# A decoder layer in one kernel: the cross-attention mask as three bf16 rows of the key and query stacks

## The reference

```python
# self attention
scores = einsum('bhqd,bhkd->bhqk', q, k) / sqrt(16)
scores = scores + log_pen[:, None, :, :]
ctx = einsum('bhqk,bhkd->bhqd', softmax(scores), v)
# cross attention (mask has the shape 4 x 1 x 1 x 512, one value per key)
logits = einsum('bhqd,bhkd->bhqk', q, k) / sqrt(16)
logits = logits + mask * -1000000000.0
ctx = einsum('bhqk,bhkd->bhqd', softmax(logits), v) @ Wo + bo
# whole layer
x = layernorm(x + self_attention(x))
x = layernorm(x + cross_attention(x, ctx_1024))
x = layernorm(x + ffn(x))
```

## Time and profile before

| what | value |
|---|---|
| timed runs, median of 3 | 867.48 us (865.65 to 867.61) |
| profiled execution, own time | 860.73 us |
| its span, first to last instruction | 858.9 us |
| mean granted TensorE clock | 0.916 of full speed |
| instructions | 10704 |
| HBM read, written | 36.91 MB, 14.68 MB |

### The profile page before, as it was taken

One profiled execution on the slowest core, in us unless ns is written; L12 is line 12 of the kernel. 1 busy time (PEld: TensorE's weight loads), 2 busy tenths in 40 slices (PEclk: granted clock), 3 DMA queues, 4 the chain that ended last, 5 costly groups with the idle time before them and its releaser, 6 DMA issues.

```text
span 858.9 us, 10704 instructions
## 1 busy us (share of the span) xinstructions
PE 685.7 (80%) x3348; PEld 264.3 (31%) x3350; DVE 611.4 (71%) x1576; ACT 478.6 (56%) x800; POOL 327.6 (38%) x417
## 2 busy tenths in 40 slices
PE   6077788998788799998887998987787899856662
PEld 3052223343222243443222433422222233223231
DVE  3978684675698766668967666697975577527996
ACT  3213456555455868744558686454366576944634
POOL 6103655655466404454663143563513001001314
PEclk9587899999999999999999999997899899996966
DMA  3533033120322314221223132331112220000002
GB/s 98 151 119 94 22 95 95 58 65 19 83 69 65 89 30 130 62 49 45 67 69 90 34 102 60 94 96 42 40 40 73 77 72 10 3 1 0 2 0 98
DMA packets 34887, 53.85 MB, mean 63 GB/s; under 512 B 4368, under 2 KB 25872, under 8 KB 34832
## 3 DMA queue, kind: packets, MB, share of 16 engines
q1 hardware_dynamic: 32912, 51.61, 20.9%
q10 hardware_dynamic: 1920, 1.57, 1.2%
HBM read 36.91 MB, written 14.68 MB: 60 GB/s over the span
## 4 chain that ended last, share of the span: by engine, by line
PE 44%; DVE 26%; POOL 11%; ACT 8%; issue 7%; DMA 3%; SPq 1%; ACTq 0%; POOLq 0%; DVEq 0%
PE ps L1446 10%; PE ps L1402 9%; DVE unused L931 8%; POOL probs L652 7%; PE ps L1422 6%; PE ps L1389 6%; PE ps L1305 5%; ACT probs L836 4%; PE ps L1382 2%; PE ps L1427 2%; PE ps L1426 2%; DMA KS<-parts_kc 2%; POOL rest L678 1%; DVE x L968 1%; DVE stats L953 1%
## 5 line engine op out<-in xcount | busy, mean ns | idle before, releaser
L1402 PE MATMUL ps<-KS,QS 96*128 96x512 bf16 x512 | 203.6, 399 | 83.5 <-DVE mx L931 55.6
L652 POOL TENSOR_TENSOR probs<-probs,penT 128x512 f32<-128x512 f32 x128 | 166.7, 1321 | 161.0 <-ACT probs L836 161.0
L836 ACT ACTIVATE probs<-ps 128x512 f32<-128x512 f32 x256 | 146.6, 597 | 142.6 <-PE ps L1427 103.0
L931 DVE CUSTOM_DVE_ANT_0 unused<-ps,lp 128x512 bf16<-128x512 f32 x256 | 169.9, 686 | 73.8 <-PE ps L1402 69.5
L1422 PE MATMUL ps<-QS,KS 108*128 108x512 bf16 x512 | 198.8, 393 | 12.6 <-ACT probs L836 12.6
L836 ACT ACTIVATE probs<-ps,mask_col 128x512 f32<-128x512 f32 x256 | 165.1, 688 | 55.3 <-PE ps L1422 53.7
L931 DVE CUSTOM_DVE_ANT_0 unused<-ps,mask_rest 128x512 bf16<-128x512 f32 x192 | 127.2, 685 | 49.1 <-PE ps L1402 48.8
L1402 PEld LDWEIGHTS ps<-KS,QS 96*128 96x128 bf16 x512 | 50.6, 99 | 265.6 <-DVE mx L931 183.9
L1446 PE MATMUL ps<-probs,v_s 128*32 128x512 f32 x512 | 72.4, 638 | 11.3 <-POOL probs L652 10.5
L1446 PE MATMUL ps<-probs,v_c 128*32 128x512 f32 x512 | 69.9, 619 | 0.9 <-ACT probs L836 0.9
L1422 PEld LDWEIGHTS ps<-QS,KS 108*128 108x128 bf16 x512 | 50.4, 100 | 59.9 <-ACT probs L836 30.2
(11 more groups left out here) (186 smaller groups left out, 941.9 us busy)
## 6 DMA issues: line engine op xcount, KB each, us to landing
parts_qs<-parts SPq DMA_DIRECT2D x8, 384.0 KB, 2.6
parts_ks<-parts SPq DMA_DIRECT2D x8, 384.0 KB, 3.1
QS<-parts_qs SPq DMA_DIRECT2D x16, 192.0 KB
KS<-parts_ks SPq DMA_DIRECT2D x16, 192.0 KB
parts_kc<-parts SPq DMA_DIRECT2D x8, 384.0 KB, 2.6
parts_qc<-parts SPq DMA_DIRECT2D x8, 384.0 KB, 2.9
QS<-parts_qc SPq DMA_DIRECT2D x16, 192.0 KB
KS<-parts_kc SPq DMA_DIRECT2D x16, 192.0 KB
```

What stands on the lines that cost most here:

```text
L652: g.tensor_tensor(probs[:, T % NP, :], probs[:, T % NP, :], penT[:, MUL_KT.index(kt), :], ALU.mult)\
L836: s_.activation(probs[:, T % NP, :], ps[:, EXP_BANKS[T % 3], :], ACT.Exp, bias=bias)\
L931: v.tensor_tensor_reduce(out=unused[:, i % 2, :], in0=ps[:, MAX_BANKS[i % 2], :], in1=lp[:, t, :] if kind == "s" else mask_row(b), scale=1 ...
L1402: mm(ps[:, MAX_BANKS[i % 2], :], QS[0:SK, slot, j, t * P:(t + 1) * P], KS[0:SK, slot, j, :], start=True, stop=True).then_inc(max_scores, 1)
```

## The change

The mask no longer comes in on DVE and ACT, but through the products. It is loaded once as 5 rows of 512 (four entries and a row of zeros for self attention), scaled and split into three bf16 parts by a new DVE job `mask_parts`, stored to DRAM as `mask_d`, and a seventh load per stack, from the fifth group on, puts the three rows of the group's entry into `KS` at partitions 96 to 98. `QS` has ones in these partitions, from a memset in `own_rows`. The row-max product of cross groups takes 99 rows, the exp product of all groups 111. The cross row maximum is a plain `tensor_reduce` over PSUM, the exponential has no bias. The rows of ones and of the maxima move up by three partitions (`SX`). The loads of the mask on all partitions, their tiles, their scalings and their semaphores go.

```diff
-SM = SK + PARTS * GH
+SX = SK + PARTS
+SM = SX + PARTS * GH
...
-STACK_DMAS = 2 * PARTS
+STACK_DMAS = 2 * PARTS + 1
...
-    add(("s", 0, 1), stacks=[], fetch=[("keys", 0), ("cT", 0)], tasks=[(0, 5, ("gate", 1)), ...
-    add(("s", 0, 2), stacks=[], fetch=[("queries", 0), ("xres", 0)], tasks=[...
-    add(("s", 0, 3), at=[(14, ("ln", 1))], fetch=[("mask", 0), ("xres", 1)], tasks=[(0, 13, ("pens", 1, (3,)))])
-    add(("s", 1, 0), fetch=[("masks", 1)], tasks=[(1, 11, ("k", "c", 0)), (8, 14, ("v", "c", 0))])
+    add(("s", 0, 1), stacks=[], fetch=[("mask", 0), ("keys", 0), ("cT", 0)], tasks=[(0, 5, ("gate", 1)), ...
+    add(("s", 0, 2), at=[(10, ("mask_parts",))], stacks=[], fetch=[("queries", 0), ("xres", 0)], tasks=[...
+    add(("s", 0, 3), at=[(14, ("ln", 1))], fetch=[("xres", 1)], tasks=[(0, 13, ("pens", 1, (3,)))])
+    add(("s", 1, 0), tasks=[(1, 11, ("k", "c", 0)), (8, 14, ("v", "c", 0))])
...
-    add(("s", 1, 3), at=[(15, ("mask_col",))], tasks=[(1, 6, ("q", "c", 0)), (7, 8, ("mask", 0)), (8, 14, ("gate", 2))])
+    add(("s", 1, 3), tasks=[(1, 6, ("q", "c", 0)), (8, 14, ("gate", 2))])
...
+        mask_d = nc.dram_tensor("mask_d", (B + 1, PARTS, S), BF16, kind="Internal").ap()
...
+        mask_f = sb("mask_f", [B + 1, S], F32, att)
+        mask_parts = sb("mask_parts", [B + 1, PARTS, S], BF16, att)
...
+        def stacked(n):
+            return 16 * (STACK_DMAS * (n // RING + 1) - 1)
...
+                if n >= RING:
+                    sp.wait_ge(mask_stored, 16)
+                    m_rows = mask_d[b if kind == "c" else B, :, :]
+                    sp.dma_start(KS[SK:SX, slot, :, :], m_rows.unsqueeze(1).broadcast_to((PARTS, GH, S)))\
+                        .then_inc(stack_loaded[slot], 16)
...
             for s in steps:
                 jobs = [job for slot in s.items for job in slot]
+                if s.p1 == RING - 1:
+                    sp.wait_ge(mask_made, 3)
+                    sp.dma_start(mask_d, mask_parts[:, :, :]).then_inc(mask_stored, 16)
...
-                if kind == "c" and i == 0:
-                    act.wait_ge(mask_col_made, 1)
-                bias = mask_col[:, b, i // GH:i // GH + 1] if kind == "c" else 0.0
-                s_.activation(probs[:, T % NP, :], ps[:, EXP_BANKS[T % 3], :], ACT.Exp, bias=bias)\
+                s_.activation(probs[:, T % NP, :], ps[:, EXP_BANKS[T % 3], :], ACT.Exp)\
...
-                v.tensor_tensor_reduce(out=unused[:, i % 2, :], in0=ps[:, MAX_BANKS[i % 2], :],
-                                       in1=lp[:, t, :] if kind == "s" else mask_row(b),
-                                       scale=1.0, scalar=LOW, op0=ALU.add, op1=ALU.max,
-                                       accum_out=mx[:, n % 2, t, j:j + 1]).then_inc(max_done, 1)
+                scores, top = ps[:, MAX_BANKS[i % 2], :], mx[:, n % 2, t, j:j + 1]
+                if kind == "s":
+                    ins = v.tensor_tensor_reduce(out=unused[:, i % 2, :], in0=scores, in1=lp[:, t, :],
+                                                 scale=1.0, scalar=LOW, op0=ALU.add, op1=ALU.max, accum_out=top)
+                else:
+                    ins = v.tensor_reduce(top, scores, AX.X, ALU.max)
+                ins.then_inc(max_done, 1)
...
                 elif what == "own_rows":
                     dve.wait_ge(consts, 5 + PARTS)
+                    v.memset(QS[SK:SX, :, :, :], 1.0).then_inc(own_rows_made, 1)
                     v.tensor_copy(KS[SK:SK + VC, :, :, :].rearrange("p r j n -> p j r n"),
...
+                elif what == "mask_parts":
+                    dve.wait_ge(loaded["masks"], 16 * 2)
+                    link(v.tensor_scalar(mask_f[:, :], mask_f[:, :], -1000000000.0, None, ALU.mult))
+                    for part in range(PARTS):
+                        v.tensor_copy(mask_parts[:, part, :], mask_f[:, :]).then_inc(mask_made, 1)
+                        if part < PARTS - 1:
+                            dve.wait_ge(mask_made, part + 1)
+                            link(v.tensor_tensor(mask_f[:, :], mask_f[:, :], mask_parts[:, part, :], ALU.subtract))
...
-                elif what == "mask":
-                    dve.wait_ge(loaded[f"mask{job[1]}"], 16)
-                    rows = mask_rest[:, :, :] if job[1] else mask_row0[:, :]
-                    v.tensor_scalar(rows, rows, -1000000000.0, None, ALU.mult).then_inc(mask_made, 1)
-                    dve.wait_ge(mask_made, job[1] + 1)
...
             def max_tile(n, i):
                 j, t, slot = i // NT, i % NT, n % RING
+                K = SX if groups[n][0] == "c" else SK
                 if i == 0:
-                    pe.wait_ge(stack_loaded[slot], 16 * STACK_DMAS * (n // RING + 1))
+                    pe.wait_ge(stack_loaded[slot], stacked(n))
...
-                mm(ps[:, MAX_BANKS[i % 2], :], QS[0:SK, slot, j, t * P:(t + 1) * P], KS[0:SK, slot, j, :],
+                mm(ps[:, MAX_BANKS[i % 2], :], QS[0:K, slot, j, t * P:(t + 1) * P], KS[0:K, slot, j, :],
```

More of the change, by code:

```diff
@@ L154, in make_plan @@
         tasks=[(1, 4, ("v", "s", 0)), (6, 15, ("lpB", 0))])
-    add(("s", 0, 1), stacks=[], fetch=[("keys", 0), ("cT", 0)], tasks=[(0, 5, ("gate", 1)), (4, 15, ("q", "s", 1)), (7, 15, ("pens", 1, (0,)))])
-    add(("s", 0, 2), stacks=[], fetch=[("queries", 0), ("xres", 0)], tasks=[(1, 11, ("k", "s", 1)), (0, 15, ("pens", 1, (1, 2)))])
-    add(("s", 0, 3), at=[(14, ("ln", 1))], fetch=[("mask", 0), ("xres", 1)], tasks=[(0, 13, ("pens", 1, (3,)))])
-    add(("s", 1, 0), fetch=[("masks", 1)], tasks=[(1, 11, ("k", "c", 0)), (8, 14, ("v", "c", 0))])
+    add(("s", 0, 1), stacks=[], fetch=[("mask", 0), ("keys", 0), ("cT", 0)], tasks=[(0, 5, ("gate", 1)), (4, 15, ("q", "s", 1)), (7, 15, ("pens", 1, (0,)))])
+    add(("s", 0, 2), at=[(10, ("mask_parts",))], stacks=[], fetch=[("queries", 0), ("xres", 0)], tasks=[(1, 11, ("k", "s", 1)), (0, 15, ("pens", 1, (1, 2)))])
+    add(("s", 0, 3), at=[(14, ("ln", 1))], fetch=[("xres", 1)], tasks=[(0, 13, ("pens", 1, (3,)))])
+    add(("s", 1, 0), tasks=[(1, 11, ("k", "c", 0)), (8, 14, ("v", "c", 0))])
     add(("s", 1, 1), at=[(4, ("lpB", 1, 0)), (8, ("lpB", 1, 1)), (12, ("lpB", 1, 2)), (13, ("v", "s", 1, 0))])
     add(("s", 1, 2), at=[(0, ("lpB", 1, 3)), (4, ("v", "s", 1, 1))], fetch=[("xT", 2)], tasks=[(6, 9, ("residual", 0)), (12, 15, ("ln1", 0))])
-    add(("s", 1, 3), at=[(15, ("mask_col",))], tasks=[(1, 6, ("q", "c", 0)), (7, 8, ("mask", 0)), (8, 14, ("gate", 2))])
+    add(("s", 1, 3), tasks=[(1, 6, ("q", "c", 0)), (8, 14, ("gate", 2))])
     add(("c", 0, 0), fetch=[("cT", 1)], tasks=[(0, 15, ("pens", 2, (0, 1)))])
@@ L164, in make_plan @@
     add(("c", 0, 2), tasks=[(0, 10, ("k", "s", 2)), (8, 15, ("residual", 1))])
-    add(("c", 0, 3), at=[(0, ("ln", 2))], tasks=[(5, 14, ("v", "s", 2)), (15, 15, ("mask", 1)), (0, 0, ("x1bias", 0)), (2, 13, ("ln1", 1))])
+    add(("c", 0, 3), at=[(0, ("ln", 2))], tasks=[(5, 14, ("v", "s", 2)), (0, 0, ("x1bias", 0)), (2, 13, ("ln1", 1))])
     for b in range(2, B):
@@ L327, in decoder_layer @@
         ffn.close()
-        loaded = {n: sem("loaded_" + n) for n in ("gate", "qk", "v", "keys", "queries", "masks", "xT", "cT", "xres0", "xres1", "mask0", "mask1")}
+        loaded = {n: sem("loaded_" + n) for n in ("gate", "qk", "v", "keys", "queries", "masks", "xT", "cT", "xres0", "xres1")}
+        mask_stored = sem("mask_parts_stored")
         w_loaded = [sem(f"ffn_weight_loaded{n}") for n in range(3)]
@@ L554, in fetch @@
                 elif what == "mask":
-                    sp.dma_start(mask_row0[:, :], a["mask_rows"][0]).then_inc(loaded["mask0"], 16)
-                elif what == "masks":
-                    sp.dma_start(mask_col[:, :, :], a["mask_col"]).then_inc(loaded["masks"], 16)
+                    sp.dma_start(mask_f[:, :], a["mask"]).then_inc(loaded["masks"], 16)
                     sp.dma_start(clips[:, :], a["clips"]).then_inc(loaded["masks"], 16)
-                    sp.dma_start(mask_rest[:, :, :], a["mask_rows"][1:B].rearrange("b p n -> p b n"))\
-                        .then_inc(loaded["mask1"], 16)
                 else:
```

20 lines of the change are left out of this document (5 added, 15 removed).

## The result

| | before | changed |
|---|---|---|
| median of 7 runs | 865.65 us (861.22 to 869.83) | 873.48 us (870.98 to 878.25) |
| ratio to before | | 1.0100 [1.0061, 1.0139] |
| profiled execution, own time | 860.73 us | 877.27 us |
| its span | 858.9 us | 875.5 us |
| mean granted TensorE clock in it | 0.916 | 0.903 |

Slower, by 8.7 us by the ratio (5.3 to 12.0), where 10.3 were forecast. So the two traces may be compared place by place, but their difference must not be read as the effect of the change.

What follows compares the result with a forecast made beforehand. No engine is simply full; the chain (44% PE, 26% DVE) bounds, with late DVE maxima holding up in-order PE. +8.5 + 4.0 + 0.8 - 2.3 - 0.7 = +10.3 us on a median of 867.5 gives 877.8, range 869.5 to 884.0.

Steps and rivals of the forecast that it cites:

- memset of the ones: DVE, own_rows in the prologue, ahead of the copy into KS: one element at a time, uncovered, 8.5 us added.
- mask operations: DVE, six dependent mask_parts instructions in step (s,0,2), uncovered on the chain: 4.0 us added, ends 2 and 5.
- seventh loads: SP's queue, one more load per stack: PE waits 0.4 us longer at each of two late stacks, 0.8 us added.
- exponentials without bias: ACT, cross tiles: 91 ns less on each of 25 exponentials on the chain, 2.3 us saved, ends 1 and 4.
- maxima by reduce: DVE, cross row maxima: 15 ns less for each of about 45 on the chain, 0.7 us saved, ends 0 and 3.
- Rival 1: Prologue memset on DVE runs at the neighbouring copy's pace, 4.4 us for 8.5: +6.2, 873.7 us, chance 0.14.
- the rival by which the read itself took up DVE: Each of 256 cross tiles gives back the accumulator read's 82 ns on the chain: 857.5 us, faster than before, chance 0.08.
- Rivals 3 and 4: Near zero: memset 4.4, mask_parts 2, 868.8 us, chance 0.10; bias still fetched as zero through a pointer: 880.1, chance 0.03.
- The signs named beforehand: What the new trace should show: instruction times and spacing, first maximum, PE waits at late stacks, and step lengths.
- The first maximum near 52: End of the prologue on DVE: the first row maximum, at 43.72 before, starts near 52 us behind the memset.
- The steps from (c,0,0) on: Later steps of the kernel: their length was to stay nearly unchanged.
- The last two groups: End of the kernel: the last two groups were to be 1 to 2 us shorter.

Runs made afterwards that it cites:

- the run in words: Changed kernel with the DVE memset of QS written as 4096 four-byte words instead of 8192 bf16 elements: 870.21 us, ratio to before 1.006.
- The run with both savings: Kernel before with no bias on the cross exponentials and plain reduce for cross maxima, mask left out: 856.89 us, ratio 0.9904.
- the last run: Changed kernel with a bias pointer to a column of zeros put back on the cross exponentials: 878.83 us, ratio to before 1.0162.

## Why the prediction was right, and where not

The sign, the main cause and the total held: 873.48 lies in the range of 869.5 to 884.0, 4.3 us below the 877.8. The loss by the ratio is 8.7 us against 10.3. Another 1.8 us of the gap is the base: the forecast started from a median of 867.5 over three runs, and the kernel before had 865.65 over seven and 864.2 to 865.9 beside the experiments.

| part | forecast | measured alone |
|---|---|---|
| memset of the ones | +8.5 | +9.0 |
| mask operations | +4.0 | +5.9 |
| seventh loads | +0.8 | 0 (within some 5) |
| exponentials without bias | -2.3 | -5.8 (put back: +5.4) |
| maxima by reduce | -0.7 | -1.7 (-4.1 to +0.6) |
| sum | +10.3 | +7.4 |

The measured parts add up to 7.4, within the 5.3 to 12.0 of the whole. Each of them carries 2 to 5 us of uncertainty, so the sum closes, but closely only by chance. That the total came out near is in part luck too: the mask operations were forecast 1.9 us too cheap and the savings 4.5 us too small, and the two errors pull in opposite directions.

**The memset** was right in place and in size. The choice between 4.4 us (the copy) and 8.5 (one element at a time) was decided by the row of the same operation on another engine, not by the neighbour on the same engine, and 8.56 us pass in the trace. Rival 1, the copy's pace, falls with that and with the run in words. One of the signs that the forecast named was misleading: it asked for a row of about 8.5 us, and the row says 6.88. Who trusts the row alone would have found 1.7 us missing.

**The mask operations** failed in one step: the forecast took the penalty of the earlier trace rows, 0.88 for 0.50, as the measure of what GpSimd's work does, and added 0.4 to each single-source instruction, then 4.0 as a middle. To the two subtractions it added nothing. The trace shows the multiply at 0.88, as priced, but 0.84 and 0.95 more on two conversions to bf16 and 0.95 more on a subtraction, for as long as GpSimd was at work. At 5.9 the term lies above its upper end of 5, though not beyond the interval. The chain was where it was said to be, and nothing absorbed the block.

**The exponentials** were sized too small: 5.8 us, outside their ends of 1 to 4, with an interval (2.7 to 8.9) that excludes the 2.3 but not the 4. The run with both savings supports it: 8.3 us (5.7 to 10.9) where 3.0 were forecast for the two. The 91 ns were right. What failed is the step of counting the exponentials that the chain of one trace shows (25) and leaving it at that. At least one effect lies outside such a count: 1.6 us in step (s,2,2), a drop of the granted clock that is in the traces of all three kernels with the bias (before, before with the plain reduce, changed with the bias put back: 24.7 us) and in none of the eleven traces without (23.1). Another 0.5 us or so lies in each of the steps (s,2,1) and (s,3,1), 20.5 us with the bias and 20.0 without. With the 2.3 that makes 4.9 at most, since the count already holds some exponentials of these steps. The last microsecond I can't place; it is within the interval of the run. Why the clock falls in that step is open as well: the runs show only that the bias, 0.3 us more standstill of PE in the step before and the drop go together, in both directions.

**The reduce** had the mechanism right: read and custom instruction occupied 0.61 us together, the reduce is spaced 0.60, and the rival by which the read itself took up DVE (857.5 us) is out. Whether 0.7 or 1.7 us or nothing was saved can't be told at this size.

**The loads** cost less than was forecast, or nothing. The forecast rightly saw that the mask rows become what PE waits for, but not that the wait stays as long as it was: 9.1 us with them, 9.0 before, 10.7 in the run without them.

**Rivals 3 and 4.** Near zero needed the memset at 4.4, which it was not. A bias that is still fetched would have left 688 ns, which only the last run shows, with the pointer put back by hand.

**The signs named beforehand.** The first maximum near 52 (52.37), all exponentials at 597, the reduce at 682 and 0.60 apart held. The mask operations took 6.3 us together, not 3.3 to 5, and PE's waits at the late stacks did not grow by 0.3 to 0.5 us each. The steps from (c,0,0) on "nearly unchanged" did not quite: (s,2,2) lost 1.6 us. The last two groups were said to be 1 to 2 us shorter, and the traces show 0.5.

## What to carry to other kernels

An addition is free only if its engine is idle there and nothing that another engine needs is queued behind it for as long as it lasts. An engine that is half idle in a step can still stall the rest of it by one block of 6 us, where PE has two tiles of slack: place such a block where the engine has one long wait, or split it over the slots (not tried here). Here the two additions cost 14.9 us (9.0 + 5.9) where they stood; moved to where engines waited, they left a kernel 0.5 to 0.6% faster than before.

Price an instruction by the distance between its neighbours rather than by its own row, and by what runs beside it. Where two profiles differ by more than their medians do, look at a stretch that the change doesn't touch before explaining anything.
